# The last three steps of a pipelined adapter kernel written out, and the order of four engines' queues changed in all its steps

## The reference, cut to what matters

```
h = gelu(x @ W_down[role] + b_down[role])          # 1024 -> 512
y = x + h @ W_up[role] + b_up[role]                # 512 -> 1024
out = (y - mean(y)) / sqrt(var(y) + 1e-5) * gamma[role] + beta[role]
```

## Time and profile before

| | us |
|---|---|
| median of 3 runs | 2741.23 (2740.98 to 2743.66) |
| profiled execution | 2742.87 |
| its span, first to last instruction | 2741.1 |
| TensorE busy | 2682.4 (98%) |
| VectorE busy | 2200.2 (80%) |
| ScalarE busy | 1668.7 (61%) |
| GpSimd busy | 1375.2 (50%) |
| mean granted TensorE clock | 0.996 |

### The profile page before, as it was taken

The page is one execution under the profiler, slowest core; times in us unless marked ns, Lnnn a source line. Parts: engine busy times, 40 slices in busy tenths (PEclk is TensorE's granted clock), DMA queues, the critical chain, the costliest instruction groups (busy, mean ns, idle before and its releaser), DMA issues.

```text
span 2741.1 us, 54380 instructions
## 1 busy us (share of the span) xinstructions
PE 2682.4 (98%) x11720; PEld 2200.6 (80%) x11720; DVE 2200.2 (80%) x3360; ACT 1668.7 (61%) x2906; POOL 1375.2 (50%) x1050
## 2 busy tenths in 40 slices
PE   8999999998999999999989999999989999999996
PEld 6888888887888888888778888888768888888885
DVE  6777777779777777777898888888888888888886
ACT  5656656666656665666656665665656565665664
POOL 1455455555545555555444454554445455545545
PEclk9999999999999999999999999999999999999999
DMA  6656566566666656656766566666766666666664
GB/s 221 219 198 219 200 209 211 202 233 223 222 205 204 209 205 209 212 201 225 235 200 220 187 222 203 206 214 201 242 197 214 199 223 191 222 204 203 214 193 149
DMA packets 360737, 573.36 MB, mean 209 GB/s; under 512 B 40162, under 2 KB 239970, under 8 KB 359394
## 3 DMA queue, kind: packets, MB, share of 16 engines
q1 hardware_dynamic: 358850, 554.14, 61.5%
q10 hardware_dynamic: 1440, 15.47, 1.6%
HBM read 364.97 MB, written 204.47 MB: 208 GB/s over the span
## 4 chain that ended last, share of the span: by engine, by line
PE 87%; DVE 6%; issue 5%; ACT 1%; DMA 1%; POOL 1%; DVEq 1%; ACTq 0%; POOLq 0%; SPq 0%
PE pD L537 46%; PE bX L549 23%; PE bZ L549 18%; DVE wul L907 1%; DVE xt L1015 1%; DVE hl L997 1%; DVE xT L968 0%; DVE xt L1007 0%; DMA rwu<-in_Wu 0%; DVE xt L1038 0%; DVE hT L982 0%; DVE xl L975 0%; DVE wdl L888 0%; POOL cs L486 0%; POOL cs L488 0%
## 5 line engine op out<-in xcount | busy, mean ns | idle before, releaser
L537 PE MATMUL pD<-wdh,xh 128*128 128x512 f32 x2080 | 811.6, 390 | 13.7 <-DVEq L959 10.1
L478 POOL TENSOR_TENSOR xt<-xt,cgb 128x1024 f32<-128x1024 f32 x258 | 630.1, 2443 | 364.8 <-ACT xt L729 364.8
L537 PE MATMUL pD<-wdh,xl 128*128 128x512 f32 x2080 | 810.4, 390 | 0.0
L537 PE MATMUL pD<-wdl,xh 128*128 128x512 f32 x2080 | 810.1, 389 | 0.0
L486 POOL TENSOR_TENSOR cs<-hT 128x256 f32<-128x256 f32 x130 | 150.7, 1159 | 910.6 <-DVE hT L982 910.6
L721 ACT ACTIVATE pC<-xt,nmean 128x512 f32<-128x512 f32 x520 | 359.8, 692 | 257.7 <-DVE nmean L1023 248.9
L729 ACT ACTIVATE xt<-xt,rstd 128x1024 f32<-128x1024 f32 x258 | 297.1, 1152 | 307.4 <-POOL rstd L471 303.9
L537 PEld LDWEIGHTS pD<-wdh,xh 128*128 128x128 f32 x2080 | 391.0, 188 | 100.3 <-DVEq L959 13.3
L537 PEld LDWEIGHTS pD<-wdh,xl 128*128 128x128 f32 x2080 | 391.0, 188 | 81.6
L537 PEld LDWEIGHTS pD<-wdl,xh 128*128 128x128 f32 x2080 | 391.1, 188 | 80.8
L549 PE MATMUL bX<-wuh,hh 128*128 128x512 f32 x1040 | 406.8, 391 | 18.2 <-DVE xt L1007 10.5
(11 more groups left out here) (119 smaller groups left out, 3830.5 us busy)
## 6 DMA issues: line engine op xcount, KB each, us to landing
xq<-in_xB SPq DMA_DIRECT2D x130, 512.0 KB, 3.6
htok<-hg SPq DMA_DIRECT2D x260, 256.0 KB, 2.9
hq<-htok SPq DMA_DIRECT2D x1040, 64.0 KB, 2.2
xt<-in_x SPq DMA_DIRECT2D x130, 512.0 KB, 4.2
mid<-xt SPq DMA_DIRECT2D x130, 512.0 KB, 3.7
xq<-mid SPq DMA_DIRECT2D x520, 128.0 KB, 3.1
xt<-mid SPq DMA_DIRECT2D x130, 512.0 KB, 4.6
out<-xt SPq DMA_DIRECT2D x128, 512.0 KB, 3.0
```

The costliest lines, as they stand in the source:

```text
L478: eng.tensor_tensor(xt[:, k, :], xt[:, k, :], cgb[:, 1, :], ALU.add).then_inc(s_o, 1)
L537: last = eng.matmul(pD[e][:, :], a[:, e, 128 * k:128 * k + 128], w[:, k, :], start=False, stop=(k == 7 and n == 2), skip_group_check=True)
```

## The change

1. All steps: the order of the SP, ScalarE and VectorE queues is another, and GpSimd tells that gamma and beta are there (`s_cg`) before `sums` and not behind it. No instruction is added or left out in these steps.
2. The steps 130, 131 and 132 of TensorE, ScalarE and VectorE are written out as `only_up(127)`, `only_up(128)` and `last_up(129)`. P5 of these three pairs goes to a bank of the product down (`pD`), which is free then, so that it waits no more for onto 4, and `seed_z` waits for onto 4 in place of onto 6.
3. The last pair takes its products in the order P0 P5 P2 P1 P3 P4 P6, and its mean and variance come from VectorE's `bn_stats` and `bn_aggr`, half by half, and not from `mean` and ScalarE's squares. `norm_last` is one instruction instead of two a slot.

The diff, cut to its core:

```diff
 SP step(i)
                 load_h(v, 0)
                 store_h(v, 1)
+                load_rows(w, 0)
+                load_h(v, 1)
                 if not (i + 1).first():
                     load_blocks(i + 1, 1)
-                load_h(v, 1)
-                load_rows(w, 0)
-                load_rows(w, 1)
-                store(z, 0)
-                store_h(i, 0)
-                if not (i + 1).first():
-                    load_blocks(i + 2, 0)
-                store(z, 1)
-                kinds.when_new(u, gains)
...
+                kinds.when_new(u, gains)
+                load_rows(w, 1)
+                store(z, 0)
+                store(z, 1)
+                store_h(i, 0)
+                if not (i + 1).first():
+                    load_blocks(i + 2, 0)
 TensorE, new (last_up; only_up keeps the order P0 to P6, with P5 as here)
+            def last_up(u):
+                X, Y = bX[u.c % 2], pD[u.c % 2]
+                product(u, 0, 0, X)
+                count(eng, s_hl, u, 4, 4)
+                count(eng, s_v, u + -2, 7, 6)
+                product(u, 5, 5, Y, True)
+                count(eng, s_v, u, 7, 1)
+                product(u, 2, 2, X)
+                count(eng, s_sz, u, 1, 1)
+                product(u, 1, 1, bZ)
+                count(eng, s_v, u, 7, 4)
+                product(u, 3, 4, bZ)
+                product(u, 4, 3, X)
+                count(eng, s_v, u, 7, 6)
+                product(u, 6, 6, X)
 ScalarE, order of a step after the change (u = i-3, w = i-2; "new" = only with new weights)
+  begin(i): high_x(i,1); new take_wu_2(u); high_h(w,0); gelu(i-1,1); seed_d(i,1)
+  end(i):   high_h(w,1); normal(u-1,0); gelu(i,0); new take_wu_0(w); high_x(i+1,0); seed_x(w); normal(u-1,1);
+            seed_d(i+1,0); new take_wd_0(i+1); high_h(w,2); seed_z(w); high_h(w,3); square(u,0,0), (u,0,1), (u,1,0);
+            new take_wd_1(i+1); square(u,1,1)
-  begin(i): high_x(i,1); gelu(i-1,1); seed_d(i,1); high_h(w,0); new take_wu_2(u)
-  end(i):   high_h(w,1); new take_wu_0(w); normal(u-1,0); high_x(i+1,0); gelu(i,0); high_h(w,2); seed_d(i+1,0);
-            normal(u-1,1); new take_wd_0(i+1); seed_x(w); seed_z(w); square(u,0,0), (u,0,1); high_h(w,3);
-            new take_wd_1(i+1); square(u,1,0), (u,1,1)
 VectorE, order of a step after the change
+  begin(i): onto 1; transpose_h(w,0); new take_wd_1(i); ready(i,wd1); transpose_h(w,1); onto 2; low_x(i,1); onto 3;
+            variance(u-1); new take_wu_2(u); ready(u,wu2); scale(u-1,0); onto 4; low_h(w,0); scale(u-1,1);
+            transpose_x(i+1,0); onto 5; new take_wu_0(w); low_x(i+1,0); ready(w,wu0); onto 6; mean(u,0)
+  end(i):   transpose_x(i+1,1); onto 7; new take_wd_0(i+1); ready(i+1,wd0); new factors(i-1); new take_wu_1(w);
+            low_h(w,1); mean(u,1); low_h(w,2); ready(w,wu1); low_h(w,3)
-  begin(i): onto 1; new take_wd_1(i); ready(i,wd1); transpose_h(w,0), (w,1); low_x(i,1); onto 2; low_h(w,0); onto 3;
-            new take_wu_2(u); ready(u,wu2); variance(u-1); scale(u-1,0), (u-1,1); onto 4; transpose_x(i+1,0);
-            onto 5; new take_wu_0(w); ready(w,wu0); low_x(i+1,0); onto 6; mean(u,0)
-  end(i):   new take_wd_0(i+1); ready(i+1,wd0); low_h(w,1); transpose_x(i+1,1); low_h(w,2); onto 7; mean(u,1);
-            new factors(i-1); new take_wu_1(w); ready(w,wu1); low_h(w,3)
 VectorE, new, the last steps
+            def only_up(u):
+                onto(u, 1, X, 0, 0)
+                transpose_h(w, 0)
+                onto(u, 2, bZ, 1, 1)
+                transpose_h(w, 1)
+                low_h(w, 0)
+                onto(u, 3, X, 0, 1)
+                variance(z)
+                last_onto(u, 4, bZ, 0, 1, 3)
+                last_onto(u, 5, X, 1, 1, 2)
+                low_h(w, 1)
+                last_onto(u, 6, Y, 0, 0, 1)
+                low_h(w, 2)
+                mean(u, 0, 6)
+                scale(z, 0)
+                ready(w, s_wu[0])
+                low_h(w, 3)
+                scale(z, 1)
+                ready(w, s_wu[1])
+                last_onto(u, 7, X, 1, 0, None)
+                mean(u, 1, 7)
+            def last_up(u):
+                ready(u, s_wu[2])
+                onto(u, 1, X, 0, 0)
+                last_onto(u, 2, Y, 0, 0, 1)
+                stats(u, 0, 0, 2)
+                onto(u, 3, X, 0, 1)
+                variance(z)
+                scale(z, 0)
+                onto(u, 4, bZ, 1, 1)
+                scale(z, 1)
+                last_onto(u, 5, bZ, 0, 1, 3)
+                stats(u, 0, 1, 5)
+                moments(0, 2)
+                last_onto(u, 6, X, 1, 1, 4)
+                stats(u, 1, 1, 6)
+                centre(u, 0)
+                last_onto(u, 7, X, 1, 0, None)
+                stats(u, 1, 0, 7)
+                moments(1, 5)
+                finish(u, 0)
+                centre(u, 1)
+                finish(u, 1)
```

More of the change, by code:

```diff
@@ L713, in square @@
             def square(u, e, m):
-                if u.exists():
+                if u.exists() and not u.last():
                     b = u.c % 2
@@ L749, in begin @@
                     high_x(i, 1)
-                gelu(i + -1, 1)
-                if not i.first():
-                    seed_d(i, 1)
                 if (i + -2).first():
                     take_wu_2(Pair(0))
-                high_h(i + -2, 0)
                 if i.first():
@@ L759, in begin @@
                     kinds.when_new(i + -3, take_wu_2)
+                high_h(i + -2, 0)
+                gelu(i + -1, 1)
+                if not i.first():
+                    seed_d(i, 1)
             def end(i):
@@ L774, in end @@
                     high_x(i + 1, 0)
-                gelu(i, 0)
-                high_h(w, 2)
+                if (i + -1).first():
+                    take_wu_0(Pair(0))
+                kinds.when_far(i + 2, load_down)
+                seed_x(w)
+                normal(u + -1, 1)
                 if not (i + 1).first():
                     seed_d(i + 1, 0)
-                normal(u + -1, 1)
                 if not (i + 1).first():
                     kinds.when_new(i + 1, take_wd_0)
-                seed_x(w)
+                high_h(w, 2)
@@ L783, in end, with only_up @@
+                square(u, 0, 0)
                 seed_z(w)
-                square(u, 0, 0)
+                high_h(w, 3)
                 square(u, 0, 1)
-                high_h(w, 3)
+                square(u, 1, 0)
                 if not (i + 1).first():
                     kinds.when_new(i + 1, take_wd_1)
+                square(u, 1, 1)
+            def only_up(u):
+                w, z = u + 1, u + -1
+                high_h(w, 0)
+                high_h(w, 1)
+                high_h(w, 2)
+                seed_x(w)
+                high_h(w, 3)
+                square(u, 0, 0)
+                kinds.when_new(u, take_wu_2)
+                square(u, 0, 1)
+                kinds.when_near(w, load_up)
+                kinds.when_new(w, take_wu_0)
+                normal(z, 0)
+                normal(z, 1)
+                seed_z(w)
@@ L789, in end @@
                 square(u, 1, 0)
                 square(u, 1, 1)
-                if (i + -1).first():
-                    take_wu_0(Pair(0))
-            steps(eng, halves(begin, end), -1, NPH + 5, 0, 5, 5)
+            def last_up(u):
+                kinds.when_new(u, take_wu_2)
+                normal(u + -1, 0)
+                normal(u + -1, 1)
+            steps(eng, halves(begin, end), -1, NPH, 0, 5, 5)
+            end(Pair(NPH - 1))
+            gelu(Pair(NPH - 1), 1)
+            only_up(Pair(NPH - 3))
@@ L796, in _ @@
+            only_up(Pair(NPH - 2))
+            last_up(Pair(NPH - 1))
         @block.vector
@@ L1087, in begin @@
                     take_wu_1(Pair(0))
+                variance(u + -1)
                 kinds.read(i + 1)
-                onto(u, 2, bZ, 1, 1)
-                low_h(w, 0)
-                if u.last():
-                    variance(u + -1)
-                onto(u, 3, X, 0, 1)
                 if not u.first():
@@ L1096, in begin @@
                 ready(u, s_wu[2])
+                scale(u + -1, 0)
+                last_onto(u, 4, bZ, 0, 1, 3)
                 kinds.when_near(w, factors)
[L1098 to L1102 removed]
+                low_h(w, 0)
                 scale(u + -1, 1)
[L1104 removed]
                 transpose_x(i + 1, 0)
```

139 lines of the change are left out of this document (88 added, 51 removed).

## The result

The changed kernel took 2750.04 us, median of 11 runs (2743.53 to 2759.92), against 2742.91 for the kernel before in the same runs: ratio 1.0030, interval 1.0022 to 1.0038. It is slower by some 8 us; 2724 was forecast. The profiled execution took 2750.58, with a span of 2748.8 against 2741.1.

A forecast was written before the change was run, and what follows sets the result against it. TensorE, 98% busy, was taken as the bound, losing time at new weights and in the last three steps. Terms -7.1 -14.5 +5.6 +1.5 +1.0 -4.2 sum to -17.7 us, giving 2724 us, range 2709 to 2738.

The forecast's parts named there:

- new W_down: Steps 30, 65, 95: onto 2 ahead of low_x and transpose_h ahead of the low parts gain 7.1 of 9.4 us lost.
- new W_up: Steps 33, 67, 68, 97 to 99: VectorE's three passes take 3.8 us instead of 8.0; 14.5 us gained of 33.8 lost.
- back edges, layer 2: VectorE's loop: D00's ready, behind transpose_x and onto 7, comes 0.7 us late on each of 8 plain edges, +5.6.
- ScalarE's edges 1.0, SP's gains 0.5: ScalarE's loop edges add 1.0 us; SP's gains(u) holding back load_rows(w,1) until the shift is done adds 0.5.
- head: First three steps: high_x(1,0) behind gelu(0,0) and seed_d(2,0) behind take_wu_0 cost +1.0 us together, bounds 0 and 3.
- steps 100, 101: Two steps given no term of their own; what the new order delays in plain steps was put at 0.
- last three steps: Steps 130 to 132: P5 no longer waits for onto 4; from step 130 to the end 48.7 us for 52.9, -4.2.
- plain step: Steps without new weights: SP's later loads and stores cost 0, covered by TensorE's own 20.4 us.
- low chance for slower: VectorE's back edge: the instruction fetch takes 2.2 us longer than counted, giving 2758 us; chance 0.07.
- order gains nothing: Rival at new weights: VectorE has the same passes and is full, so 0 for the 21.6 us, 2745 us; chance 0.13.

The follow-up runs named there:

- e1: The changed kernel with SP's step in its order of before, everything else changed: 2731.95 us, ratio 0.9966 to the kernel before.
- e10: On e1, low_h 1 of VectorE's end put ahead of transpose_x and onto 7 everywhere: 2737.35 us, ratio 0.9979 to the kernel before.
- e5: On e1, take_wd_0 and the ready for D00 put ahead of transpose_x and onto 7 again: 2737.90 us, ratio 0.9985 to the kernel before.
- e9: On e1, last three steps: seed_z and last pair's ready earlier, VectorE's scales and ScalarE's squares moved: 2730.84 us, ratio 0.9959 to the kernel before.
- e12: On e1, only load_blocks(i+1,1) put behind load_h(v,1) and load_rows(w,0), as in the changed kernel: 2761.08 us, ratio 1.0062 to the kernel before.

## Why the prediction was wrong

Terms in us. "Alone" is e1 against the kernel before, in the profiled executions (sums of the steps' excess); the last column is what the changed kernel adds to e1.

| term | predicted | alone | with SP's order |
|---|---|---|---|
| new W_down: 30, 65, 95 | -7.1 | -4.5 | +6.5 |
| new W_up: 33, 34, 67 to 70, 97 to 99 | -14.5 | -13.9 | +3.1 |
| back edges, layer 2 | +5.6 | +5.7 | -1.9 |
| ScalarE's edges 1.0, SP's gains 0.5 | +1.5 | 0 | not told apart |
| head | +1.0 | -2.0 | +7.8 |
| steps 100, 101 | 0 | 0 | +6.5 |
| last three steps | -4.2 | +1.5 | -0.9 |

The column "alone" adds up to 13.2, and by the ratios of many runs the gain is 9.3. The last column adds up to 21, and by the ratios it is 17.5. No step of e1 outside the rows of the table has an excess, so nothing of the 1.0 for ScalarE's edges was paid.

**The step that failed** is the plain step's: load_blocks(i+1,1) and load_h "are issued around S+11 and want to land by S+16.7", "store_h(i,0) and load_blocks(i+2,0) now stand behind store(z,1) at S+19; nobody wants them before the next step's 12th us. I cost all this at 0". For a plain step the walk was right: load_blocks(i+1,1) was put at S+11 and goes out near S+10.5, and plain steps take 20.4. The mistake was to walk SP's queue there and nowhere else. At new weights each call waits longer: the pair of stores ahead of step 94's calls was held 11 us, load_h waited twice, and the load left at S+20.2. What was put at 0 measured 17.5 us by the ratios of e1 and the changed kernel. The same paragraph says that "without the cover each us late is a us a step", and nothing in it asks where the cover is thin. The range's low chance for slower came from VectorE's edge alone; no rival had SP in it, and SP's part in the sum was 0.5 us for gains(u).

**The head** is in part scatter. Step 3 starts at 57.9 in the changed kernel and at 50.1 in e1, 7.8 us apart. ScalarE's high_x of pair 2, changed kernel and below it e1:

```profile
37.55 1.06 ACT L706 ACTIVATE xh<-xq 128x1024 fp32r<-128x1024 f32 x1 [0.56 <-DMA xq<-in_xB]
46.93 1.06 ACT L706 ACTIVATE xh<-xq 128x1024 fp32r<-128x1024 f32 x1 [4.06 <-DMA xq<-in_xB]
```

```profile
33.65 1.06 ACT L706 ACTIVATE xh<-xq 128x1024 fp32r<-128x1024 f32 x1 [1.23 <-DMA xq<-in_xB]
38.92 1.04 ACT L706 ACTIVATE xh<-xq 128x1024 fp32r<-128x1024 f32 x1
```

The first starts 3.9 us later, and everything behind it with it: four copies of W_up from 38.5 and seed_d(2,0) at 42.3, for which TensorE waited 5.9 (1.9 at this place in e1). But its block was issued at 26.0 in both. Over all runs that block is issued at 25.9 to 26.5 and high_x starts at 33.5 to 37.6, with SP's order of before too: e10 has 36.4 and starts step 3 at 55.6. So this half isn't shown to be SP's order. The second half is: load_blocks(2,1) was issued at 43.2 instead of 34.6, and high_x(2,1) waited 4.1 us for it. With SP's order of before, step 3 starts at 50.1 to 53.5 in all runs but e10 (52.0 in the kernel before), so the table's 7.8 is some 4 too much for the order. The +1.0 had only ScalarE's order in it.

**New W_up** was right in size, -13.9 against -14.5, and in part by luck. The new wait of P1 for low_h 1 came as forecast (2.2 us at step 68, 2.1 walked). But the wait of P4 for take_wu_2 was 0.4 in e1's step 68 where 2.0 was walked, and D00 of step 68 had none where 1.0 was walked. In their place P1 of step 67 waited 1.4, and the granted clock fell to 0.50 once behind P1 in each of the steps 33, 68 and 98, for 3.4 us, in which seven or eight matmuls follow each other every 0.427 us instead of 0.227: about 1.6 us each. The walk had counted none, "since no wait reaches 2.8"; the waits of P1 before these falls are 2.6, 2.2 and 2.2. The kernel before has one such fall in each of these steps too, so they are no part of the gain. The rival "order gains nothing" falls.

**New W_down** gave 4.5 of 7.1: in e1 steps 30 and 65 keep 0.8 and 2.2, where 0.4 was taken for each, and 95 keeps 2.0, where 1.5 was.

**The back edges**: 0.8 to 1.1 us on each of eight in e1, on six of eight in the changed kernel, against 0.7, and none in the first layer, by a wrong cause. Ready stood at S+2.05 in the walk, behind the end of onto 7. In e1 it came at S+1.40, although transpose_x started 0.7 later than walked: it didn't wait for either to finish (see the last section). The instruction that was late is low_h 1, whose place behind mean the same paragraph had read off and then dropped. e5 and e10 tell the two apart. A right number didn't make a right reason: an edit built on it (e5) lost 5 us by the ratios.

**The tail** was mis-sized by 5.7 in e1 and by 4.8 in the changed kernel (53.5 against 48.7). The waits that were walked for P1, P5, P3 and P6 came, those for P0 of both pairs didn't. The walk had P1 of pair 128 at t = 14.8; it came at 14.7 (2710.00 less 2695.27), 3.6 us late for seed_z, not 2.3:

```profile
2710.00 0.47 PE L552 MATMUL bZ<-wuh,hh 128*128 128x512 f32 x1 [3.58 <-issue]
2724.30 0.47 PE L552 MATMUL pD<-wuh,hh 128*128 128x512 f32 x1 [2.86 <-DVEq L1035]
2731.60 0.50 PE L552 MATMUL bZ<-wuh,hh 128*128 128x512 f32 x1 [1.33 <-DVE xt L1083]
2735.93 0.50 PE L552 MATMUL bX<-wuh,hh 128*128 128x512 f32 x1 [1.28 <-DVE xt L1091]
```

The clock, which the walk left out, fell behind the first two (0.92 over the 42 us, 0.96 before):

```profile
2711.50:2714.80 3.30, 3.30 (x9) 2.63 (x8) 2.20 (x4) 0.30 (x1) 3.14 (x4) 0.50 0.44 178
2725.20:2728.50 3.30, 3.30 (x10) 2.54 (x9) 1.39 (x3) 1.30 (x4) 2.90 (x2) 0.50 0.41 164
```

Each of these two stretches costs 1.6 us, eight matmuls at 0.427; the kernel before has one in its tail. So P0 of pair 129 came at 24.6, as walked, but behind the slow matmuls and not behind ready. P5 came at 29.0 instead of 27.2. The waits of P3 and P6, 1.3 us each, are what the walk had for them, but they came at 36.3 and 40.7 instead of 32.8 and 36.7. The last product ended 42 us after step 130's start, as before, not 38.1. Then VectorE's first centre met the shift. VectorE and, below it, GpSimd in the changed kernel:

```profile
2736.52 3.30 DVE L1131 SCALAR_TENSOR_TENSOR xt<-xt,mv,cgb 128x1024 f32<-128x1024 f32 x1
2739.75 0.68 DVE L1091 SCALAR_TENSOR_TENSOR xt<-bX,xt 128x512 f32<-128x512 f32 x1
...
2742.86 1.28 DVE L1131 SCALAR_TENSOR_TENSOR xt<-xt,mv,cgb 128x1024 f32<-128x1024 f32 x1
```

```profile
2734.05 4.69 POOL L481 TENSOR_TENSOR xt<-xt,cgb 128x1024 f32<-128x1024 f32 x2 [1.26 <-ACT xt L777]
```

The same instruction takes 3.30 beside a shift and 1.28 without one, and onto 7 behind it came some 2 us late. The chain that ended last runs through this centre, onto 7, the second centre and the finishes, not through pair 128's stores as walked. The prediction had weighed the rule of the Trainium skill (SBUF — State Buffer, Who interferes with whom) only for the passes of take_wu_1. Here the measured 3.47 in e9 and 3.30 agree with it to 0.2 us: 1.28 and the rest of a shift of 2.4.

What stays open: why the late load costs 9 us more beside the old stores (e12), what the pair of stores costs by itself with the load late, and why the first block of pair 2 lands up to 4 us later in some executions. It wasn't tried to issue load_blocks from another engine's queue.

## What to carry to other kernels

When calls are reordered in the queue that issues the transfers, walk it through the fullest step, not the plain one: a load that went out some 8 us ahead of its use in a plain step came too late where two large stores had held the queue and a weight fetch ran beside it, and moving the one line back gave 15 us. Give every load its own place ahead of calls that wait for something unrelated (here for a transpose and a landed store). And before an edit is built on a reason, check which instruction TensorE's wait names, even if the size came out right.
